# Gated attention with experts: other counts at which the scatters wait, the experts' count earlier, the variance's root earlier

## The chip, the core and the metric

The kernel runs on one core of one Trainium2 chip. The metric is the device time of one execution in microseconds (us). A core has TensorE (PE, matrix products), VectorE (DVE), ScalarE (ACT), GpSimd (POOL) and SyncE (SP), each with its own queue of instructions that run in order, and 16 DMA engines. Engines tell one another of finished work by semaphores.

## What is computed

The input x is 8 batches of 512 rows of 256. Attention here runs over the 256 features, not over the rows, and its result gates with a mixture of 32 experts, 6 of them for each row:

```
xn = layernorm(x)
q, k, v = xn Wq, xn Wk, xn Wv
scores  = einsum('bse,bsf->bef', q, k) / sqrt(8)       # 256 x 256 for each batch
s       = (softmax(scores) applied to v) Wo
logits  = xn gate_weight^T                             # 32 experts
        softmax; best 3 of 8 groups; best 6 experts of them; their weights normalised
y       = sum over a row's 6 experts of weight * (silu(xn w1^T) * (xn w3^T)) w2^T
shared  = (silu(xn sw1^T) * (xn sw3^T)) sw2^T
out     = x + s * silu(y + shared)
```

## The kernel before

There are two stages. In the first, a loop over the 8 batches computes the attention, the shared expert and the routing, and writes each normalised row to six places of a table in HBM, `slots_d`, sorted by expert. The second runs over pairs of pages of 128 such rows through the experts, gathers the results back and writes the output. The change touches the first stage only. Batches are numbered 0 to 7 here, as `b` in the code.

The order on every engine is written out by hand. TensorE's `batch(b)` (L736) runs, in this order: half of the shared expert's first layer (`shared_up(0)`, L718, semaphore `s_ab_ps`); the product A (L710, `s_a_ps`); `shared_up(1)`; the turning of the next batch's rows (`turn`, L685, `s_xt_ps`); the scores S (L710, `s_s_ps`); the next batch's logits (`gate`, L698, `s_lg_ps`); half of the shared expert's second layer (L726, `s_y_ps`); the product R (L710, `s_r_ps`), which waits for the softmax's weights (ACT, L533, `s_p`); the other half (L726, `s_y_ps`); the product M (L710, `s_m_ps`), which waits for ACT's copy of R (L602); the next batch's Gram matrix (`gram`, L732); `count(b + 1)` (L704 and L705, `s_cnt`), which counts the chosen experts of the next batch from `sel16`, VectorE's result of the routing (L920, `s_sel`); and last the attention's output (L726 into banks 2 and 3, `s_at_ps`), which waits for ACT's copy of M (L610).

VectorE's `batch(b)` (L1064): the shared expert's hidden values (L1044), the scores' maximum (L1068), the next but one batch's statistics (L877), then `route(b + 1)` (from L925, which waits for the logits), `split_low` (L995), `low_weights(b - 1)` (12 instructions on L1050), `spread_root(b + 2)` and `moved_mean` (L887 to L898, which finish the inverse root of the variance), `place(b + 1)` (from L949, which waits for `s_cnt`) and `weigh(b + 1)`. ScalarE normalises the next but one batch's rows (L527) as soon as L898 is done; those stand in its queue ahead of L610.

GpSimd issues the scatters, indirect DMAs of 128 rows each, on L487: 24 for each batch, 192 in all. It numbers those of one batch n = 0 to 23. Before some of them `let_pass(b, n)` (L463) waits until TensorE has reached a certain product. No data need these waits.

```
due = {4: (s_y_ps, 2 * b + 1), 7: (s_r_ps, b + 1), 9: (s_y_ps, 2 * b + 2),
       11: (s_m_ps, b + 1), 15: (s_at_ps, 2 * b + 2)}
if nxt:
    due.update({2: (s_lg_ps, b + 2), 13: (s_cnt, b + 2), 17: (s_ab_ps, HC * b + HC + 1),
                19: (s_a_ps, b + 2), 21: ...})
```

So ahead of scatter 7 of batch b, POOL waits for R of batch b. The ones at 17, 19 and 21 wait for products of the next batch.

## Time and profile before

| | us |
|---|---|
| median of 3 executions | 685.56 |
| lowest and highest | 684.07 and 687.75 |
| profiled execution, its time | 691.99 |
| profiled execution, its span | 690.2 |
| PE, DVE, ACT, POOL busy in the span | 548.6, 472.2, 359.1, 383.4 |

The profile is of one execution, whose own time lies 6.43 us above the median. Its span, 690.2 us, is what the trace covers; 1.8 us lie around it. Times in the rows are us from the span's start. The first stage ends on TensorE at about 304 us. In a row of the timeline, the number in brackets is how long the engine had been idle before the instruction, and behind the arrow stands what ended that; "remote" there means that a semaphore's update came at that moment, well after the instruction that made it had ended.

### The profile page before, as it was taken

To read this page: it belongs to the slowest core of one execution; us is meant where nothing else is said; L and a number is where in the kernel's file an instruction comes from. 1 tells how busy PE (TensorE), PEld (TensorE's weight loads), DVE (VectorE), ACT (ScalarE), POOL (GpSimd) and SP (SyncE) were. 2 spreads that over 40 slices of the span, in tenths; PEclk is the share of its full clock that TensorE was granted. 3 is DMA by queue.
4 is the path that set the end of the run, shared out by engine and by line. 5 is a ranking of instruction groups with operands and counts; after the bars stand their busy time and mean duration, and the time that the engine had idled before them with its cause. 6 is when DMAs were issued, how large, how long until landed. Compare 5 with 4: busy or idle time off the path is not lost.

```text
span 690.2 us, 14473 instructions
## 1 busy us (share of the span) xinstructions
PE 548.6 (79%) x4095; PEld 446.7 (65%) x4095; DVE 472.2 (68%) x1443; ACT 359.1 (52%) x606; POOL 383.4 (56%) x402
## 2 busy tenths in 40 slices
PE   7789696979697978437999889888888889888830
PEld 6566575756576765326999777777777777677620
DVE  6968687877788877722454567667677667667765
ACT  5546464546464644224655656556556556556421
POOL 1156667676666766753003556556565556565662
PEclk9889798998898999868999999999999999999975
DMA  9999996858393532754888888888888988888764
GB/s 320 416 354 347 366 334 227 285 214 298 130 334 113 207 117 91 230 150 122 201 217 262 290 280 283 280 280 285 290 272 292 279 279 267 290 276 286 226 198 141
DMA packets 111288, 174.80 MB, mean 253 GB/s; under 512 B 25072, under 2 KB 68848, under 8 KB 110320
## 3 DMA queue, kind: packets, MB, share of 16 engines
q1 hardware_dynamic: 87280, 108.29, 47.4%
q0 software_dynamic: 18432, 50.36, 23.2%
q10 hardware_dynamic: 5504, 15.24, 6.4%
q8 instruction: 40, 0.66, 0.4%
q14 instruction: 32, 0.26, 0.1%
HBM read 78.41 MB, written 92.27 MB: 247 GB/s over the span
## 4 chain that ended last, share of the span: by engine, by line
PE 53%; DVE 21%; issue 15%; another core or an unknown queue 6%; ACT 4%; DMA 1%; DVEq 0%; SPq 0%; ACTq 0%
PE ps L835 17%; PE ps L857 8%; PE ps L726 7%; PE ps L710 6%; PE ps L818 6%; PE ps L718 4%; DVE sw L1133 3%; PE ps L845 3%; PE ps L732 2%; DVE w_all L1050 2%; DVE work L1152 2%; DVE work L1159 1%; DVE stats L877 1%; DVE early L1141 1%
## 5 line engine op out<-in xcount | busy, mean ns | idle before, releaser
L508 POOL DMA_INDIRECT early<-slots_d,slot_at x192 | 186.6, 972 | 178.0 <-DMA slots_d<-early 56.6
L487 POOL DMA_INDIRECT slots_d<-early,slot_at x96 | 96.9, 1009 | 75.0 <-issue 25.7
L487 POOL DMA_INDIRECT slots_d<-work,slot_at x96 | 97.7, 1018 | 45.1 <-issue 26.5
L835 PE MATMUL ps<-w_all,xnT 128*128 x798 | 102.9, 275 | 15.9 <-issue 13.6
L835 PEld LDWEIGHTS ps<-w_all,xnT 128*128 128x128 f16 x798 | 71.4, 98 | 36.3 <-issue 24.6
L647 ACT ACTIVATE xnT<-ps 128x1024 f16<-128x1024 f16 x67 | 68.8, 1029 | 46.6 <-PE ps L818 28.0
L668 ACT ACTIVATE early<-ps 128x512 f32<-128x512 f32 x112 | 67.3, 602 | 46.6 <-remote 30.8
L818 PE MATMUL ps<-ident,work 128*128 128x128 f16 x796 | 66.7, 222 | 24.9 <-issue 24.8
L1159 DVE CAST work<-ps 128x256 f16<-128x256 f32 x75 | 31.6, 422 | 75.0 <-remote 45.0
L1133 DVE SCALAR_TENSOR_TENSOR sw<-early,wk,sw 128x256 f32<-128x256 f32 x160 | 77.7, 486 | 3.5
L818 PEld LDWEIGHTS ps<-ident,work 128*128 128x128 f16 x796 | 54.6, 99 | 28.8 <-issue 26.4
L653 ACT ACTIVATE work<-ps 128x256 f32<-128x256 f32 x112 | 43.9, 393 | 55.6 <-remote 37.9
L857 PE MATMUL ps<-w_all,work 128*128 x447 | 62.6, 277 | 0.9 <-issue 0.9
L1152 DVE SCALAR_TENSOR_TENSOR work<-ps,work 128x256 f32<-128x256 f32 x112 | 46.5, 416 | 20.4 <-ACT work L653 19.0
L710 PE MATMUL ps<-early,work 128*128 128x256 f32 x128 | 39.4, 462 | 25.8 <-ACT work L533 18.9
L835 PE MATMUL ps<-w_all,sw 128*128 x396 | 50.6, 274 | 8.3 <-issue 8.0
L710 PEld LDWEIGHTS ps<-early,work 128*128 128x128 f32 x128 | 28.6, 231 | 34.7 <-ACT work L533 21.0
L726 PE MATMUL ps<-work,early 128*128 128x256 f32 x128 | 34.7, 432 | 17.7 <-issue 13.8
L857 PEld LDWEIGHTS ps<-w_all,work 128*128 128x128 f16 x447 | 43.9, 99 | 6.3 <-issue 1.5
L835 PEld LDWEIGHTS ps<-w_all,sw 128*128 128x128 f16 x396 | 35.4, 98 | 18.6 <-issue 12.7
L647 ACT ACTIVATE sw<-ps 128x1024 f16<-128x1024 f16 x33 | 34.0, 1032 | 20.9 <-remote 15.4
L718 PE MATMUL ps<-xnT,sw 128*128 128x512 f16 x192 | 44.0, 379 | 0.0
(164 smaller groups left out, 989.4 us busy)
## 6 DMA issues: line engine op xcount, KB each, us to landing
slots_d<-early SPq DMA_DIRECT2D x112, 256.0 KB
work<-slots_d SPq DMA_DIRECT2D x100, 256.0 KB
slots_d<-pad SPq DMA_DIRECT2D x7, 3072.0 KB
w_all<-in_wexp ACTq DMA_DIRECT2D x7, 1536.0 KB
slots_d<-work SPq DMA_DIRECT2D x1, 5120.0 KB, 19.2
s_all<-in_x SPq DMA_DIRECT2D x8, 512.0 KB, 6.3
ysh_d<-work ACTq DMA_DIRECT2D x8, 512.0 KB
early<-ysh_d SPq DMA_DIRECT2D x32, 128.0 KB
```

The lines of the kernel that those rows point to most:

```text
L487: pool.indirect_dma_start(slots_d[:, :], bass.IndirectOffsetOnAxis(ap=slot_at[:, at:at + 1], axis=0), split[b % XN_RING][:, t, :], None).t ...
L508: pool.indirect_dma_start(gath[:, at % GATH_RING, :], None, slots_d[:, :], bass.IndirectOffsetOnAxis(ap=slot_at[:, rank_of(at):rank_of(at) ...
L647: act.activation(x_halves[n % 3], turned_pair(p), ACT.Copy).then_inc(s_eT, 1)
L668: act.activation(y_e[:, p % DEEP, :], ps[:, 2 + p % 2, :], ACT.Copy, scale=1.0 / W_UP).then_inc(s_ey, 1)
L710: mm = pe.matmul(ps[:, bank, m * H:(m + 1) * H], lhs[:, k, m * P:(m + 1) * P], rhs[:, k, :], start=(k == 0), stop=(k == HC - 1))
L718: mm = pe.matmul(ps[:, 4 + 2 * m + w, :], sw13[:, w_low, w, k, m * P:(m + 1) * P], xnT16[:, x_low, k, :], start=(n == 0 and k == 0), stop= ...
L726: mm = pe.matmul(ps[:, bank + n, t * H:(t + 1) * H], lhs[:, k, at:at + P], rhs[:, k, :], start=(k == 0), stop=(k == HC - 1))
L818: mm = pe.transpose(turned_pair(p)[:, at:at + P], slot16[:, at_slot(p) + h, low, c * P:(c + 1) * P], ident16[:])
L835: mm = pe.matmul(ps[:, 5 + p % 2, h * 2 * I:(h + 1) * 2 * I], turned_x(p)[:, x_low * HC + k, h * P:(h + 1) * P], w16[:, bass.ds(at + (w_lo ...
L857: mm = pe.matmul(ps[:, 2 + p % 2, h * H:(h + 1) * H], hT_e[p % 3][:, h_low, h, :], w16[:, bass.ds(at + (w_low * WEXP + HC * 2 * I), H)], s ...
L1133: dve.scalar_tensor_tensor(acc[:, k, :], gath[:, at % GATH_RING, :], wk[:, rank_of(at):rank_of(at) + 1], ysh_l[k] if at % TOP_K == 0 else ...
L1152: dve.scalar_tensor_tensor(h_e[p % 2], up(p)[:, :, 1, :], 1.0 / (X_UP * W_UP), silu_e[p % 2], ALU.mult, ALU.mult).then_inc(s_eh, 1)
```

## The change

Three places are edited. The waits of POOL's scatters get other counts: from batch 1 on there are six a batch instead of ten, for R, M, the attention's output, and the next batch's A, S and logits. In batch 0 the waits ahead of 17, 19 and 21 become one, for the second half of `shared_up` of batch 1. On TensorE `count(b + 1)` moves from behind the Gram matrix to ahead of M. On VectorE `low_weights` moves behind the variance's root.

```diff
-                nxt = b + 1 < B
-                due = {4: (s_y_ps, 2 * b + 1), 7: (s_r_ps, b + 1), 9: (s_y_ps, 2 * b + 2),
-                       11: (s_m_ps, b + 1), 15: (s_at_ps, 2 * b + 2)}
-                if nxt:
-                    due.update({2: (s_lg_ps, b + 2), 13: (s_cnt, b + 2), 17: (s_ab_ps, HC * b + HC + 1),
-                                19: (s_a_ps, b + 2), 21: (s_xt_ps, 2 * b + 6) if b + 2 < B else (s_a_ps, b + 2)})
+                if b == 0:
+                    due = {2: (s_lg_ps, 2), 4: (s_y_ps, 1), 7: (s_r_ps, 1), 9: (s_y_ps, 2), 11: (s_cnt, 2),
+                           13: (s_m_ps, 1), 15: (s_at_ps, 2), 17: (s_ab_ps, HC + HC)}
                 else:
-                    due[2] = (s_s_ps, b + 1)
+                    due = {3: (s_r_ps, b + 1), 7: (s_m_ps, b + 1), 13: (s_at_ps, 2 * b + 2)}
+                    if b + 1 < B:
+                        due[17] = (s_a_ps, b + 2)
+                if b + 1 < B:
+                    due[20] = (s_s_ps, b + 2)
+                if b + 2 < B:
+                    due[23] = (s_lg_ps, b + 3)
...
                 half_by_tile(1, 6, hT_s, sw2, s_y_ps)
+                if not last:
+                    count(b + 1)
                 pe.wait_ge(s_r, b + 1)
                 product(1, w_vT, r_s, s_m_ps)
                 if not last:
                     gram(b + 1, 0)
                     gram(b + 1, 1)
-                    count(b + 1)
...
                 split_low(b + 1)
-                if b >= 1:
-                    low_weights(b - 1)
                 if b + 2 < B:
                     spread_root(b + 2)
                     moved_mean()
+                if b >= 1:
+                    low_weights(b - 1)
                 place(b + 1)
```

POOL's queue before, from the first scatter of batch 2; the names behind "waits" are the semaphores that the instruction waits for (`s_split`, `s_pads2` and `s_slots` guard its data, the others stand there through `let_pass`):

```order
67 L487 DMA slots_d<-early,slot_at 28672x256 [waits s_split,s_pads2,s_slots]
68 L487 DMA slots_d<-early,slot_at 28672x256
69 L487 DMA slots_d<-early,slot_at 28672x256 [waits s_lg_ps]
70 L487 DMA slots_d<-early,slot_at 28672x256
71 L487 DMA slots_d<-early,slot_at 28672x256 [waits s_y_ps]
72 L487 DMA slots_d<-early,slot_at 28672x256
73 L487 DMA slots_d<-early,slot_at 28672x256 [waits s_split]
74 L487 DMA slots_d<-early,slot_at 28672x256 [waits s_r_ps]
75 L487 DMA slots_d<-early,slot_at 28672x256
76 L487 DMA slots_d<-early,slot_at 28672x256 [waits s_y_ps]
77 L487 DMA slots_d<-early,slot_at 28672x256
78 L487 DMA slots_d<-early,slot_at 28672x256 [waits s_m_ps]
```

The same place in POOL's queue of the changed kernel, from the scatter of batch 1 that waits for the logits; L490 is L487 of before:

```order
59 L490 DMA slots_d<-work,slot_at 28672x256 [waits s_lg_ps]
60 L490 DMA slots_d<-early,slot_at 28672x256 [waits s_split,s_pads2,s_slots]
61 L490 DMA slots_d<-early,slot_at 28672x256 x2
62 L490 DMA slots_d<-early,slot_at 28672x256 [waits s_r_ps]
63 L490 DMA slots_d<-early,slot_at 28672x256 x2
64 L490 DMA slots_d<-early,slot_at 28672x256 [waits s_split]
65 L490 DMA slots_d<-early,slot_at 28672x256 [waits s_m_ps]
66 L490 DMA slots_d<-early,slot_at 28672x256 x4
67 L490 DMA slots_d<-early,slot_at 28672x256 [waits s_split]
68 L490 DMA slots_d<-early,slot_at 28672x256 [waits s_at_ps]
69 L490 DMA slots_d<-early,slot_at 28672x256 x3
70 L490 DMA slots_d<-early,slot_at 28672x256 [waits s_a_ps]
```

R's wait moved from the eighth scatter of a batch to the fourth, M's from the twelfth to the eighth, and the logits' from the third of a batch to the last of the one before it.

VectorE's queue before, at the end of batch 1's part:

```order
179 L995 SCALAR_TENSOR_TENSOR early<-early 128x256 x4
180 L1050 SCALAR_TENSOR_TENSOR w_all<-w_all 128x256 x12
181 L887 RECIPROCAL rough<-std 128x4
182 L888 SCALAR_TENSOR_TENSOR newt<-rough 128x4
183 L889 SCALAR_TENSOR_TENSOR newt<-mv,newt 128x4
184 L890 SCALAR_TENSOR_TENSOR rstd<-newt,rough 128x4
185 L898 SCALAR_TENSOR_TENSOR shift<-mv,rstd 128x4
186 L947 MEMSET early 128x32
187 L949 COPY counts<-ps 128x4x32
```

And of the changed kernel:

```order
179 L999 SCALAR_TENSOR_TENSOR early<-early 128x256 x4
180 L891 RECIPROCAL rough<-std 128x4
181 L892 SCALAR_TENSOR_TENSOR newt<-rough 128x4
182 L893 SCALAR_TENSOR_TENSOR newt<-mv,newt 128x4
183 L894 SCALAR_TENSOR_TENSOR rstd<-newt,rough 128x4
184 L902 SCALAR_TENSOR_TENSOR shift<-mv,rstd 128x4
185 L1054 SCALAR_TENSOR_TENSOR w_all<-w_all 128x256 x12
186 L951 MEMSET early 128x32
187 L953 COPY counts<-ps 128x4x32
```

The five small instructions of the root now stand ahead of the twelve of the low weights; the copy of the counts keeps its place.

## Rows read from the trace of the kernel before

**Rows 1.** Windows, batches 1 to 6 and batch 7: busy us and instructions by engine.

```profile
54.30:263.00 208.70, 173.42 (x782) 133.10 (x781) 162.68 (x603) 114.11 (x181) 142.00 (x141) 0.89 0.71 244
263.00:304.40 41.40, 23.72 (x90) 16.78 (x88) 23.86 (x72) 15.14 (x20) 26.98 (x28) 0.79 0.54 171
```

**Rows 2.** Waits, 40 to 310 us: us in total, times, longest.

```profile
POOL slots_d L487 <- remote: 22.3, 11, 3.4
...
DVE counts L949 <- issue: 16.3, 5, 6.6
...
ACT early L527 <- DVE shift L898: 13.8, 5, 5.0
```

**Rows 3.** Timeline, batch 1, R and M: start, us, engine, line, [idle before].

```profile
71.49 1.99 PE L710 MATMUL ps<-early,work 128*128 128x256 f32 x8 [1.19 <-issue]
...
72.30 0.96 POOL L487 DMA_INDIRECT slots_d<-work,slot_at  x1 [0.30 <-issue]
...
74.15 0.29 DVE L920 TENSOR_TENSOR sel<-early 128x128 bf16<-128x128 f32 x1
...
76.16 1.04 POOL L487 DMA_INDIRECT slots_d<-work,slot_at  x1 [0.30 <-issue]
78.91 0.60 ACT L602 ACTIVATE work<-ps 128x512 f32<-128x512 f32 x1 [3.87 <-remote]
79.16 1.73 POOL L487 DMA_INDIRECT slots_d<-work,slot_at  x1 [1.96 <-remote]
...
79.56 3.78 PE L710 MATMUL ps<-work,early 128*128 128x256 f32 x8 [4.36 <-issue]
```

**Rows 4.** Timeline, batch 2, product R, POOL's stop ahead of scatter 7, product M.

```profile
106.94 2.42 PE L710 MATMUL ps<-early,work 128*128 128x256 f32 x8 [2.56 <-issue]
...
114.59 2.53 POOL L487 DMA_INDIRECT slots_d<-early,slot_at  x1 [1.83 <-remote]
...
115.00 3.62 PE L710 MATMUL ps<-work,early 128*128 128x256 f32 x8 [2.66 <-issue]
```

**Rows 5.** Timeline, batch 3, product M and the attention's output.

```profile
147.77 1.89 PE L710 MATMUL ps<-work,early 128*128 128x256 f32 x8
147.88 1.04 POOL L487 DMA_INDIRECT slots_d<-work,slot_at  x1 [0.31 <-issue]
...
156.43 0.96 POOL L487 DMA_INDIRECT slots_d<-work,slot_at  x1 [2.30 <-remote]
...
156.84 6.74 PE L726 MATMUL ps<-work,early 128*128 128x256 f32 x16 [3.61 <-ACT work L610]
```

**Rows 6.** Timeline, batch 4, the logits and product R.

```profile
172.93 1.87 PE L698 MATMUL ps<-g_w,early 128*128 128x32 f32 x16
173.13 0.96 POOL L487 DMA_INDIRECT slots_d<-work,slot_at  x1 [0.30 <-issue]
...
179.62 0.29 DVE L925 TENSOR_REDUCE row<-ps 128x4 f32<-128x128 f32 x1 [3.11 <-remote]
179.86 0.96 POOL L487 DMA_INDIRECT slots_d<-early,slot_at  x1 [1.97 <-remote]
...
183.04 3.78 PE L710 MATMUL ps<-early,work 128*128 128x256 f32 x8 [6.44 <-ACT work L533]
```

**Rows 7.** Timeline, batch 7 and the first pair of pages.

```profile
282.79 1.89 PE L710 MATMUL ps<-work,early 128*128 128x256 f32 x8
...
288.69 0.96 POOL L487 DMA_INDIRECT slots_d<-work,slot_at  x1 [0.30 <-issue]
...
298.07 0.95 POOL L487 DMA_INDIRECT slots_d<-work,slot_at  x1 [3.38 <-remote]
...
298.48 5.90 PE L726 MATMUL ps<-work,early 128*128 128x256 f32 x16 [13.80 <-issue]
...
312.21 1.86 PE L818 MATMUL ps<-ident,work 128*128 128x128 f16 x16 [7.72 <-issue]
...
316.77 0.96 POOL L487 DMA_INDIRECT slots_d<-work,slot_at  x1 [0.30 <-issue]
```

## The prediction

> **What bounds the kernel now.** Read the windows first. Batches 1 to 6 take 208.7 us, 34.8 us each; TensorE is busy for 173.42 of them, 28.9 a batch, so some 5.9 us a batch are holes in it [rows 1]. No other engine fills a batch either: VectorE is busy 27.1 us of it, ScalarE 19.0. POOL shows 142.00 us for 141 scatters, 1.007 us each, and between two that wait for nothing stand 0.30 us [rows 1, 3]. So 24 scatters need 24 x 1.31 = 31.4 us of a batch's 34.8: POOL has 3.4 us to spare and no more.
>
> Next the waits and the timeline, to see what the holes are. In the first stage POOL alone ends 11 waits, 22.3 us, on "remote" [rows 2], a semaphore that came long after its instruction. The reader is to compare three times in each stretch: when the product ended, when its reader started, and when POOL last stopped. In batch 1 the product R ended at 71.49 + 1.99 = 73.48. ScalarE, idle and next in line, copied it only at 78.91, 5.4 us later; POOL had issued scatters all the while, stopped at 77.20 for R's semaphore itself (its wait ahead of scatter 7), and the copy came 1.7 us behind that stop [rows 3]. Batch 2 repeats it: R ended at 109.36, POOL stopped at 112.76, went on at 114.59, M started at 115.00 after 2.66 us of idling [rows 4]. In batch 3 it is M: ended at 149.66, POOL stopped ahead of scatter 11 at 154.13, released at 156.43 [rows 5]. In batch 4 the logits: ended at 174.80, stop at 177.89, VectorE's first reader at 179.62 [rows 6]. In batch 7 M ended at 284.68, POOL stopped at 294.69 and was released at 298.07; TensorE idled 13.80 us [rows 7]. So **an update of TensorE's that falls into a run of scatters may be seen only 1.7 to 3.4 us after POOL stops**. It does not always happen: M of batch 2 is no such case. What `let_pass` sets is therefore where POOL stops, and the question is whether it stops before the product ends or after.
>
> TensorE also pays behind a hole: M took 3.78 and 3.62 us after holes of 4.36 and 2.66 [rows 3, 4] and 1.89 without one [rows 5], so it ran there at half of the full clock, 1.2 for 2.4 GHz. The attention's output took 6.74 us after 3.61 [rows 5]. The Trainium skill, in "TensorE: Matmul & The Clock Gate", part 1, says that the clock depends on how busy the array has been of late and falls to half when it idles. By that rule alone a closed hole gives more than its length; the trace agrees, with 3.78 against 1.89.
>
> **The change part by part.**
>
> *R's wait from scatter 7 to 3, M's from 11 to 7.* In batch 1 scatter 3 is the one at 72.30 [rows 3]; POOL would have stood still from 72.00, before R's end at 73.48. The hole of 4.36 closes and M runs at 1.89 instead of 3.78: 6.2 us. In batch 2 the stop moves four scatters, 5.2 us, ahead, from 112.76 to 107.5, before R's end: 2.66 + 1.73 = 4.4 us. In batch 3 scatter 6, at 147.88, would be the last and end at 148.92, before M's end at 149.66: the 3.61 close and 6.74 halves, 7.0 us. In batch 7 scatter 6 is the one at 288.69, so the stop comes at 289.65 instead of 294.69; M ended before either, so its update stays late, but by 5.0 us less [rows 7].
>
> *The logits' wait from scatter 2 of the next batch to 23.* In batch 4 scatter 22 is the one at 173.13; POOL would stop at 174.09, before the logits end at 174.80. VectorE's 3.11 us of idling go, and with them that much of TensorE's 6.44 [rows 6]: 3.1 us. Batches 5 and 6 I credit with nothing.
>
> These sum to 6.2 + 4.4 + 7.0 + 3.1 = 20.7 us ahead of batch 7 and 5.0 in it. But the sum assumes that POOL stays where it was, and it can't: it has only 3.4 us a batch, 20.5 us in six. Were TensorE to gain all of it, POOL would never be early for anything. **Counts against time** show where it would be late. From R to M TensorE needs two products at 1.89, 3.8 us, and POOL has four scatters to issue, 5.2 us: 1.5 us late. From S to the logits TensorE needs 1.87 us and POOL three scatters, 3.9 us: 2.1 late. Only from the logits to R, where TensorE waits for the softmax (from 174.80 to 186.8 in batch 4, and 8 to 9 us if nothing is late), does it have time to spare for four, 5.2 us. So some updates get caught as now, with 1.7 us behind the stop. Bounds for batches 1 to 6: 0, if each closed hole opens another, and 20.5. I take the middle, 10, since the rows show R certain to profit and M and the logits now and then. With 5.0 in batch 7 this is 15.
>
> *Waits removed (both for the shared expert's second layer, its first, the counts, the turned rows).* A wait that is passed costs nothing; one that stops POOL costs it up to 2.30 us [rows 5]. Their removal lets POOL run on over these signals. What they release (ScalarE's copy of the shared output, ahead of R's copy in its queue) must be out before R, and POOL now stops for R. Cost 0; bounds 2.3 us a batch either way, one such stop more or less. *The new wait for S* holds POOL at scatter 20 near the moment when S ends; behind it are queued only scatters, and behind their landing in the end the next but one batch's split rows (ScalarE L539). Cost 0, the same bounds.
>
> *The count between R and M.* Two small products move, with their wait for `s_sel`. Queued behind are M and all after it. In batch 1 `sel16` was ready at 74.44, and TensorE was through with what precedes the count at 79.56 - 4.36 = 75.20: a slack of 0.8 us [rows 3]. A faster R would eat it. Cost 0 to 1 us a batch; I take 0.5 in all, because M waits for R's copy anyway. The gain: VectorE waited 16.3 us in five batches for the counts [rows 2], 3.3 each. Its later results reach TensorE only through the hidden values and the next batch's scores; in the rows TensorE idles for ScalarE or a late semaphore. Gain 0 to 3.3 a batch; I take 0.5 in all.
>
> *The root ahead of the low weights.* ScalarE waited 13.8 us in five batches for it [rows 2], 2.8 each. No DMA moves with it. It feeds the next but one batch's rows; of TensorE's work it delays only the copy of M, queued behind, which the Gram matrix covers. Gain 0 to 2.8 a batch, taken as 0. The low weights come five small instructions later, and ScalarE needs them only at the batch's end: 0. If that cover is gone, the 2.8 are on the path and add to the gain.
>
> **Sum**: 691.99 - 15 + 0.5 - 0.5 = 677.0 for the profiled execution. It lies 6.43 us above the median 685.56. Nothing tells what these 6.4 are, but late updates are what can differ from one execution to the next at an unchanged program, so I expect the median execution to have a third fewer of them, and the change to give it two thirds: 10. That makes 675.6.
>
> **The rivals.** *POOL becomes the bound and it gets slower.* The mechanism is the late stop itself: each of the six waits that catches an update costs POOL about 1.9 us [rows 3, 4]. With n of them in a batch it takes 31.4 + 1.9 n. At n = 1.8 that is today's 34.8, the point from which it decides; at n = 3 it is 37.1, 2.3 more, 14 us in six batches. Less the 5 of batch 7 and a little elsewhere, 8 us: 693. For it: two of the six waits are late by the counts above, and 11 scatters instead of 9 remain behind TensorE's last product of the stage. Against it: today there are ten waits. Those two scatters, 2.6 us, end later than the 317.73 of now; the pairs of pages that need them come well behind the first at 312.21 [rows 7].
>
> *The waits don't matter.* Updates are late by chance, and moving a stop moves the chance. Then only VectorE's and ScalarE's edits are left, 0 to 2 us: 684. The Trainium skill, in "Advanced Engine Details and Errata", Miscellaneous Facts, gives 50 to 100 ns for a sequencer's reading of a semaphore. By that figure no product would be seen microseconds late and this rival would be right. The rows speak against it: in five stretches the delay ends 1.7 to 3.4 us behind POOL's stop, wherever that is.
>
> *All of it is gained*: 20.5 + 5.0, at two thirds 17, or whole 25.5: 660 to 668. It needs POOL never to wait in vain, and two of the counts speak against it.
>
> **How the numbers follow.** The forecast, 668 to 682, has 0.55; all of it 0.15; the waits don't matter, 682 to 689, 0.17; slower 0.13. Likeliest is 675.6. The range of 8 in 10 runs from 664 to 689, leaving out the slow case and the lower part of the best. A measurement of this kernel can tell about 0.5%, 3.4 us, from no change: faster 0.70, same 0.17, slower 0.13.
>
> **What would show it.** Right: the timeline has POOL idle ahead of scatter 3 when R ends, and ScalarE's copy of R within 0.3 us of that; M takes 1.9 us in most batches; batches 1 to 6 take near 33 us; TensorE's idling ahead of batch 7's output is 8 to 9 us instead of 13.80. Wrong: the holes ahead of M are closed but those ahead of the logits' or A's readers have grown; TensorE idles ahead of the moved count; batches stay at 34.8. The forecast fails if an update is held by something other than POOL's scatters.

## The result: no gain, slightly slower

The changed kernel takes 692.31 us (688.09 to 697.30, 22 runs), the kernel before beside it 689.20 us (684.07 to 694.95, 22 runs): ratio 1.0045, 95% interval 1.0023 to 1.0067. The forecast of 675.6 and its range, 664 to 689, both miss it. The profiled execution took 697.3 us, its span is 695.6; before it was 691.99 and 690.2. The profiled execution is the slowest of the 22, so the two profiles lie further apart (5.4 us) than the medians (3.1 us). Each profile is one execution; where a single hole falls can differ from one to the next.

### The profile after

Lines moved by 3 or 4: scatters are L490, products L713, halves of the outputs L729, the logits L701, the count L707, the first reader of the logits L929. First the windows of batches 1 to 6 and of batch 7 (us from and to, length, then busy us and instructions of TensorE, its weight loads, VectorE, ScalarE, POOL, then granted clock, DMA share, GB/s). They answer to [rows 1]:

```profile
55.70:265.20 209.50, 172.26 (x782) 132.93 (x781) 157.03 (x583) 113.51 (x180) 137.98 (x140) 0.89 0.70 239
265.20:304.30 39.10, 22.02 (x90) 15.19 (x88) 23.39 (x70) 15.52 (x21) 26.18 (x27) 0.83 0.57 178
```

The six batches take 209.5 us instead of 208.7, and the output ends at 304.3 as it did. The waits between 40 and 310 us (us in total, times, longest) answer to [rows 2]:

```profile
POOL slots_d L490 <- remote: 25.5, 15, 3.3
...
ACT s_all L622 <- remote: 19.4, 6, 5.1
...
DVE row L929 <- remote: 9.2, 3, 3.9
...
DVE mx L1072 <- remote: 8.2, 3, 3.3
...
ACT work L605 <- remote: 3.4, 1, 3.4
...
ACT early L530 <- DVE shift L902: 1.4, 2, 0.9
```

The same waits in the kernel before:

```profile
ACT work L602 <- remote: 9.9, 2, 6.0
...
DVE row L925 <- remote: 7.4, 3, 3.1
...
ACT s_all L619 <- remote: 2.3, 1, 2.3
```

VectorE's 16.3 us of waiting for the counts are down to 1.2, ScalarE's 13.8 for the root to 1.4: both edits do what they say. But VectorE now waits 21.0 us in seven stretches for ScalarE's part of the hidden values (L1048), where before it waited 0.5 us: its wait has moved as well. POOL's late releases went up, from 11 (22.3 us) to 15 (25.5). The late waits of others changed their place: ScalarE's for R (L602, now L605) fell from 9.9 to 3.4 us; those for the logits rose from 7.4 to 9.2, for S (the scores' maximum, L1072) from none to 8.2, and for the attention's output (L619, now L622) from 2.3 to 19.4. Now the timeline of batch 1, to be read beside [rows 3] (start, us, what, in brackets the idle time before and what ended it):

```profile
71.34 1.99 PE L713 MATMUL ps<-early,work 128*128 128x256 f32 x8 [2.50 <-issue]
...
76.53 0.23 PE L707 MATMUL ps<-sel,ones 128*128 128x128 bf16 x1 [1.47 <-DVE sel L924]
...
77.05 1.06 ACT L542 ACTIVATE early<-early 128x1024 f16<-128x1024 f32 x1 [5.76 <-DMA slots_d<-early,slot_at]
...
77.51 0.96 POOL L490 DMA_INDIRECT slots_d<-work,slot_at  x1 [2.14 <-remote]
...
79.13 2.56 PE L713 MATMUL ps<-work,early 128*128 128x256 f32 x8 [2.32 <-ACT work L605]
```

R ended at 73.33. POOL stood ahead of scatter 3 only from 77.51 - 2.14 = 75.37, and not from 72.00 as forecast, because its stops in batch 0 had grown and batch 1 began 3.3 us later on it. TensorE idled 1.47 us ahead of the moved count and 2.32 ahead of M, 3.8 us together instead of 4.36; M took 2.56 us instead of 3.78. Ahead of R's copy in ScalarE's queue stood L542, which waited until 77.05 for scatters to land. So in batch 1 the hole stayed. In batches 2 to 6 the hole ahead of M is gone. And this is what stands ahead of the next R, that of batch 2, to be read beside [rows 4]:

```profile
99.14 1.94 PE L701 MATMUL ps<-g_w,early 128*128 128x32 f32 x16
...
104.09 0.96 POOL L490 DMA_INDIRECT slots_d<-work,slot_at  x1 [0.30 <-issue]
...
105.92 0.29 DVE L929 TENSOR_REDUCE row<-ps 128x4 f32<-128x128 f32 x1 [3.91 <-remote]
106.16 0.96 POOL L490 DMA_INDIRECT slots_d<-work,slot_at  x1 [1.11 <-remote]
...
109.34 3.78 PE L713 MATMUL ps<-early,work 128*128 128x256 f32 x8 [6.46 <-issue]
```

The logits ended at 101.08. POOL issued scatters until 105.05, stopped ahead of scatter 23, and VectorE read them at 105.92, 4.8 us late and 0.9 us behind the stop. R waited 6.46 us (2.56 before) and ran at 1.2 GHz, 3.78 us. Over batches 1 to 6, TensorE's holes ahead of the count, M and the attention's output fell from 12.0 us to 3.8; those ahead of or within the logits and ahead of R rose from 23.3 to 33.4. The balance, 2.0 us more, is TensorE's idle time in the windows (208.70 - 173.42 = 35.3 us and 209.50 - 172.26 = 37.2). Its busy time fell by 1.2 us, so the six batches grew by 0.8. **The holes moved from one product to another.**

In batch 7, beside [rows 7]:

```profile
284.33 1.99 PE L713 MATMUL ps<-work,early 128*128 128x256 f32 x8 [0.71 <-issue]
...
291.90 0.96 POOL L490 DMA_INDIRECT slots_d<-work,slot_at  x1 [0.30 <-issue]
295.87 0.60 ACT L601 ACTIVATE work<-ps 128x512 f32<-128x512 f32 x1 [11.59 <-remote]
296.21 0.96 POOL L490 DMA_INDIRECT slots_d<-work,slot_at  x1 [3.35 <-remote]
...
299.01 5.32 PE L729 MATMUL ps<-work,early 128*128 128x256 f32 x16 [12.69 <-ACT work L613]
```

M ended at 286.3. POOL stopped for it at 292.9; the updates were seen 3.0 us later, at 295.9, when ScalarE could start on the copies ahead of M's in its queue. The stop came 1.8 us earlier than before (294.7), not 5.0, since POOL began the batch 3.3 us later. The hole shrank from 13.80 to 12.69.

Where are the 5.4 us by which the span grew? Not ahead of the output's end (304.4 and 304.3). Behind it the last scatter ended at 320.2 instead of 317.7, ScalarE's first SiLU of the experts came at 321.2 instead of 319.0, POOL's first gather at 373.9 instead of 369.8: 4.1 us of the 5.4; the other 1.3 fell behind that. The start of the experts' stage in the changed kernel (first product, POOL's last scatter, first SiLU):

```profile
314.23 2.30 PE L839 MATMUL ps<-w_all,xnT 128*128 x12 [0.45 <-issue]
...
319.23 0.96 POOL L490 DMA_INDIRECT slots_d<-work,slot_at  x1 [0.30 <-issue]
321.16 0.38 ACT L656 ACTIVATE work<-ps 128x256 f32<-128x256 f32 x1 [4.96 <-remote]
```

And in the kernel before, where the last scatter is the one at 316.77 [rows 7]:

```profile
314.53 2.47 PE L835 MATMUL ps<-w_all,xnT 128*128 x12 [0.45 <-issue]
...
318.96 0.66 ACT L653 ACTIVATE work<-ps 128x256 f32<-128x256 f32 x2 [2.46 <-PE ps L835]
```

The first product ended 0.5 us earlier (316.5 instead of 317.0), and its reader started 2.2 us later: 4.6 us late instead of 2.0, and in both kernels 1.0 to 1.2 us behind the last scatter's end. Behind POOL's last stop no stop follows in that run of scatters, so this too is a late update.

### The profile page after: what moved, and what is told of

Its sections match the earlier page's. It is cut to its first block, busy times and chain, and to the rows that moved or that the text cites. A ratio compares the mean times of both kernels' runs of the same rounds, so it can differ in the third digit from the quotient of the medians.

```text
span 695.6 us, 14473 instructions
## 1 busy us (share of the span) xinstructions
PE 554.7 (80%) x4095; PEld 443.7 (64%) x4095; DVE 469.5 (67%) x1443; ACT 358.4 (52%) x606; POOL 379.3 (55%) x402
## 4 chain that ended last, share of the span: by engine, by line
PE 49%; DVE 16%; issue 14%; another core or an unknown queue 11%; ACT 8%; DMA 1%; DVEq 0%; ACTq 0%
PE ps L839 18%; PE ps L861 8%; PE ps L713 6%; PE ps L729 5%; PE ps L822 5%; PE ps L735 4%; DVE sw L1137 4%; PE ps L849 3%; ACT w_all L561 2%; DVE work L1156 2%; DVE work L1163 1%; PE ps L721 1%; ACT L582 1%; DVE stats L881 1%
## 5 line engine op out<-in xcount | busy, mean ns | idle before, releaser
L490 POOL DMA_INDIRECT slots_d<-early,slot_at x96 | 95.4, 993 | 77.8 <-issue 25.6
L839 PE MATMUL ps<-w_all,xnT 128*128 x798 | 107.5, 276 | 29.6 <-issue 23.1
L490 POOL DMA_INDIRECT slots_d<-work,slot_at x96 | 96.5, 1005 | 47.5 <-issue 26.5
L839 PEld LDWEIGHTS ps<-w_all,xnT 128*128 128x128 f16 x798 | 69.8, 98 | 52.0 <-issue 38.8
L822 PE MATMUL ps<-ident,work 128*128 128x128 f16 x796 | 61.9, 222 | 7.5 <-issue 7.5
L713 PE MATMUL ps<-early,work 128*128 128x256 f32 x128 | 40.7, 474 | 29.7 <-ACT work L536 20.7
L839 PE MATMUL ps<-w_all,sw 128*128 x396 | 52.9, 277 | 8.9 <-issue 8.6
L1156 DVE SCALAR_TENSOR_TENSOR work<-ps,work 128x256 f32<-128x256 f32 x112 | 46.3, 413 | 16.7 <-issue 15.2
L713 PEld LDWEIGHTS ps<-early,work 128*128 128x128 f32 x128 | 29.6, 239 | 39.0 <-ACT work L536 23.7
L839 PEld LDWEIGHTS ps<-w_all,sw 128*128 128x128 f16 x396 | 33.8, 99 | 23.9 <-issue 15.7
L849 PE MATMUL ps<-ident,work 128*128 128x128 f32 x223 | 44.0, 278 | 3.2 <-issue 3.2
L729 PE MATMUL ps<-work,early 128*128 128x256 f32 x128 | 30.6, 395 | 12.7 <-ACT work L613 12.7
```

Of the source, the lines that this page charges most:

```text
L490: pool.indirect_dma_start(slots_d[:, :], bass.IndirectOffsetOnAxis(ap=slot_at[:, at:at + 1], axis=0), split[b % XN_RING][:, t, :], None).t ...
L713: mm = pe.matmul(ps[:, bank, m * H:(m + 1) * H], lhs[:, k, m * P:(m + 1) * P], rhs[:, k, :], start=(k == 0), stop=(k == HC - 1))
L729: mm = pe.matmul(ps[:, bank + n, t * H:(t + 1) * H], lhs[:, k, at:at + P], rhs[:, k, :], start=(k == 0), stop=(k == HC - 1))
L822: mm = pe.transpose(turned_pair(p)[:, at:at + P], slot16[:, at_slot(p) + h, low, c * P:(c + 1) * P], ident16[:])
L839: mm = pe.matmul(ps[:, 5 + p % 2, h * 2 * I:(h + 1) * 2 * I], turned_x(p)[:, x_low * HC + k, h * P:(h + 1) * P], w16[:, bass.ds(at + (w_lo ...
L849: mm = pe.transpose(turned_hidden(p)[:, h * P:(h + 1) * P], h_e[p % 2][:, h, :], ident[:])
```

## Experiments

The kernel before takes 689.7 us on the chip of the first runs and 694.8 to 696.4 on three others, but 590.1 and 589.4 on two. Ratios are always to the kernel before on the same chip. That difference was not foreseen and turned out useful: in the eight traces taken on the 590-us chips no wait ends on "remote", so no update of TensorE's is late there. The kernel before was timed on those chips but not profiled.

### The parts alone

The waits alone are the new `let_pass` in the kernel before; the count alone is

```
                 half_by_tile(1, 6, hT_s, sw2, s_y_ps)
+                if not last:
+                    count(b + 1)
                 pe.wait_ge(s_r, b + 1)
...
-                    count(b + 1)
```

and the root alone moves `low_weights(b - 1)` behind `spread_root(b + 2)` and `moved_mean()`.

> The kernel before with the new counts of the scatters' waits alone. Theory A (late updates only change their place: the holes ahead of M close, those ahead of R and the logits' readers open, and two more scatters are left behind the last product of the first stage, so that the first pairs of pages wait for them): all of the change's loss is here, ratio 1.003 to 1.007, and the profile has M's holes under 1 us in batches 1 to 6 and R's at 5 to 6 us. Theory B (the moved count or the moved root is what costs): ratio under 1.001.

> The kernel before with the experts' count ahead of M alone. Theory A: within 0.2% of before, since M waits for ScalarE's copy of R anyway; VectorE's waits for the counts shrink from 3.3 us each to under 1. Theory B (TensorE stands idle for sel16 ahead of the count, and M, Gram and all behind it come later): 1.5 us in each of 7 batches, ratio 1.005 or more.

> The kernel before with the variance's root ahead of the low weights alone. Theory A: within 0.2% of before; ScalarE's waits for the root fall from 2.8 us each to under 1, and nobody waits for what ScalarE does there. Theory B: the low weights, 1 us later, hold the high weights at the batch's end and so the next batch: ratio over 1.003.

Measured (kernel before 689.70): waits 694.36, 1.0070 (1.0041 to 1.0100); count 689.63, 0.9999 (0.9973 to 1.0025); root 687.83, 0.9970 (0.9939 to 1.0001). The sum of the three, +0.4%, is the whole change's 1.0045. The loss is the waits', and the root may have gained 0.3%, which its interval just fails to show. The ratio of the waits alone is at the top edge of theory A; the profile is only in part what that theory said: M still had holes of 4.1 and 2.8 us in batches 1 and 5, and R's were 0.9 to 6.2.

The profile of the waits alone holds a surprise. Its output ends at 292.9, 11 us earlier than before, and its first transposes of pages (L821) still come at 311.7, against 312.2 before:

```profile
293.24 0.27 PE L794 MATMUL ps<-ident,table 128*1 128x128 f32 x1 [0.36 <-DVE table L1032]
...
303.80 0.23 DVE L1037 CAST early<-ps 1x76 int16<-1x76 f32 x1 [8.69 <-remote]
...
311.70 1.86 PE L821 MATMUL ps<-ident,work 128*128 128x128 f16 x16 [18.19 <-issue]
```

The turned table of experts (L794), which every page's product needs, was ready at 293.5 and seen at 303.8. POOL, being behind, found the output's semaphore already there and made no stop. So a TensorE that is ahead of POOL makes the stops vanish that let its updates through.

### Does POOL hold the updates?

The kernel before without any wait in `let_pass` (nothing that is computed is left out), and the changed kernel with the old waits, so with count and root alone:

```
             def let_pass(b, n):
+                pass
...
-                if n in due:
-                    pool.wait_ge(*due[n])
```

> The kernel before without any of let_pass's waits. Theory L (updates of TensorE are held while POOL issues scatters, and the stops let them pass): holes of 10 us and more in every batch, over 750 us. Rival W (the waits are only a cost; updates are late by chance): POOL's last scatter ends some 20 us sooner, and the time falls to 670 or is unchanged.

> The changed kernel with all of its scatters' waits as before: the moved count and the moved root together. If the parts add: 0.9999 x 0.997, ratio 0.994 to 1.000, and the changed kernel's 1.0045 is the waits' 1.007 less the root's 0.003. If the count costs once the root is early: over 1.000.

These fell on a 590-us chip: no waits 588.27, 0.9964 (0.9948 to 0.9981); old waits 591.37, 1.0008 (0.9987 to 1.0029). The first again, on a chip with 696.43:

> The same kernel without any of let_pass's waits, meant for the chip on which the kernel before takes 690 us (on the one where it takes 590 no update came late). Theory L (there updates of TensorE are held while POOL issues scatters, and stops let them pass): holes of 10 us and more in most batches, over 720 us. Rival W (late by chance, the waits only cost): 680 us or less.

802.41 us, 1.1519 (1.1428 to 1.1610). Its waits, whole span:

```profile
POOL slots_d L477 <- DVE slot_at L979: 152.8, 8, 25.8
...
PE ps L700 <- ACT work L592: 61.8, 5, 17.4
```

Without a stop TensorE idles up to 17.4 us ahead of M (L700) and 20.0 ahead of the attention's output, and POOL then waits for a batch's addresses, 11.9 to 21.1 us in each of seven batches (the 25.8 is the wait at the start, 25.6 in the kernel before). The same edit gains 0.4% where the kernel before takes 590. So the late updates are real, belong to POOL's runs of scatters, occur on some chips only, and `let_pass` is worth 15% there. This part of the prediction's reasoning stands. What in a run of scatters holds an update (POOL itself or the transfers that it starts) is not shown. The old waits with the new count and root once more on a chip with 589.41:

> The changed kernel with all of its scatters' waits as before, for a chip of 690 us. If the parts add, 0.9999 x 0.997: ratio 0.994 to 1.000. If the root's gain was chance: 0.999 to 1.003.

591.55, 1.0029 (1.0016 to 1.0043): no gain from the two edits there. It was meant for a 690-us chip; there count and root together were not run.

### Which of the moved waits?

Two kernels, one with batch 0's table as before, the other with the last batch's as before, the rest as changed:

```
                 if b == 0:
-                    due = {... 9: (s_y_ps, 2), 11: (s_cnt, 2),
-                            13: (s_m_ps, 1), 15: (s_at_ps, 2), 17: (s_ab_ps, HC + HC)}
+                    due = {... 9: (s_y_ps, 2), 11: (s_m_ps, 1), 13: (s_cnt, 2),
+                           15: (s_at_ps, 2), 17: (s_ab_ps, HC + 1), 19: (s_a_ps, 2), 21: (s_xt_ps, 6)}
...
+                if b == 1:
+                    due[2] = (s_lg_ps, 3)
...
+                if b == B - 1:
+                    due = {2: (s_s_ps, B), 4: (s_y_ps, 2 * B - 1), 7: (s_r_ps, B), 9: (s_y_ps, 2 * B),
+                           11: (s_m_ps, B), 15: (s_at_ps, 2 * B)}
```

> The changed kernel with batch 0's waits as before, again for the chip of 690 us. Theory P (3 us of the loss are POOL's stop ahead of scatter 17 of batch 0): ratio 0.998 to 1.001. Theory Q (the waits for S and the logits cost): 1.004 or more. Where no update is late, as on the chip of 590 us, it was 1.0058.

> The changed kernel with the waits of the last batch as they were before (M's ahead of scatter 11 instead of 7, the output's ahead of 15 instead of 13). Theory A (the scatters left at the end delay the first pairs of pages): M's update comes up to 5 us later, but four scatters more are out by then; the first pair's updates are seen 2 to 4 us sooner counted from the stage's last product. Net ratio to before 0.998 to 1.004. If the stage's last hole alone counted (the reason of the prediction), it would be 5 us slower than the changed kernel: 1.011.

1.0071 (1.0034 to 1.0108; 703.54 against 696.43) and 1.0065 (1.0034 to 1.0096; 694.57 against 689.70): the loss stays with either, so neither end alone makes it; no run has both as before. The first is no clean test of batch 0: its stops sum to 7.4 us instead of 12.2, but batch 1, with the logits' stop ahead of scatter 2 and R's ahead of 3, stood 10.9 us instead of 4.3. (The first of the two was 1.0058, 594.21, on a 590-us chip. A table with fewer stops, ahead of 2, 5, 11, 15 and 19, was expected to give 0.985 to 1.000 and gave 1.0160, 600.29, there: POOL's stops summed to 20.2 us beyond the usual 0.30, 12.4 of them from batch 1 on, against 7.9 and none with the old waits on that chip.)

Then the two halves of the change apart, in batches 1 to 6: R, M and the output at 3, 7 and 13, the waits for the shared layer's second products and the counts gone, the others as before; and S at 20 instead of the turned rows at 21 and the logits at 23, with R and M as before.

```
+                if 1 <= b < B - 1:
+                    due = {2: (s_lg_ps, b + 2), 3: (s_r_ps, b + 1), 7: (s_m_ps, b + 1), 13: (s_at_ps, 2 * b + 2),
+                           17: (s_ab_ps, HC * b + HC + 1), 19: (s_a_ps, b + 2), 21: due[21]}
```

> The kernel before, with R's wait ahead of scatter 3, M's of 7 and the output's of 13 in batches 1 to 6, and the waits for the shared layer's second products and the counts gone there; logits, A and the turned rows as before. Where updates come late (690 us). Theory E (stopping earlier for R and M costs POOL its idling between the logits and R without an earlier R): ratio 1.004 to 1.008. Theory S (the stops for S and the logits cost): 0.995 to 1.002.

> The kernel before, with the turned rows' wait ahead of 21 replaced by S ahead of 20, and the logits' wait moved from scatter 2 to scatter 23 of the batch before. Theory S (two stops 1.9 us apart on TensorE with three scatters of 3.9 us between make the logits late each time, so the holes ahead of R are 5 to 6 us): ratio 1.004 to 1.008. Theory E: 0.997 to 1.002.

On a chip with 589.41 they gave 592.06, 1.0035 (1.0015 to 1.0054), and 593.93, 1.0084 (1.0054 to 1.0115): where nothing is late a stop only costs. The first half again, on a chip with 694.77:

> The kernel before with only the waits of R and M (and of the attention's output, 15 to 13) moved in batches 1 to 6 to scatters 3 and 7; the logits' wait stays at scatter 2, and all that were there before remain. The prediction's sum gave these two waits 17.6 us. Theory A (only POOL's total counts): R and M holes smaller, but the last scatter and the whole within 0.5% of before, or slower by up to 0.5% if POOL idles more. Theory B (it is the logits' and S's waits that spoil the change): faster by 1 to 2.5%, 0.975 to 0.99, where the kernel before takes 690; no gain where it takes 590.

717.88 us, 1.0312 (1.0234 to 1.0389): neither theory's number. (The text above says that all other waits remain; in the kernel the three ahead of 4, 9 and 13 are gone.) R and M early, which by the sum of their parts were to bring 17.6 us, cost 23. Batch 1's end in it:

```profile
96.80 1.94 PE L701 MATMUL ps<-g_w,early 128*128 128x32 f32 x16 [0.83 <-ACT early L547]
...
105.84 0.96 POOL L490 DMA_INDIRECT slots_d<-early,slot_at  x1 [0.30 <-issue]
109.05 0.29 DVE L928 TENSOR_REDUCE row<-ps 128x4 f32<-128x128 f32 x1 [9.38 <-remote]
109.29 0.96 POOL L490 DMA_INDIRECT slots_d<-early,slot_at  x1 [2.49 <-remote]
```

The logits ended at 98.74, when 19 of the batch's scatters were out; before it were 21 to 23. The stop for them stands ahead of scatter 2 of the next batch, and they were seen at 109.05, 10.3 us late; so in each of five batches, 9.6 to 10.3 us late (VectorE's waits for it are 9.4 us at most, 37.6 in all), and TensorE idled 8.8 to 10.5 us ahead of R. POOL, stopped again one scatter later for R itself, stood there for 4.3 to 6.3 us. Its stops in batches 1 to 6 sum to 49.4 us beyond the usual 0.30, instead of 23.1. An earlier stop moves TensorE ahead of POOL for all that comes after. The waits alone, which have stops at 20 and 23, cost 0.7% instead of 3.1% (on another chip, and with other tables in batches 0 and 7), so those stops seem to mend most of this, and not all: S ends when 17 to 19 of POOL's scatters are out instead of 19 to 22, and its stop is at 20. S and the logits early were not run on such a chip, so what that half does alone there is open.

### What takes the gain at the end?

Without the last eight scatters of the last batch (those eight row groups are left out of the computation):

```
+                        if b == B - 1 and t * TOP_K + k >= 16:
+                            continue
```

> The kernel before without the last 8 of batch 7's 24 scatters; their rows are missing from the table. Theory P (the first pairs' updates are held till POOL's last scatter ends, so the experts' stage starts by that and not by TensorE's last product): ScalarE's first silu follows the last scatter by 1 to 2 us still, up to the 10 us that TensorE needs behind its last product, and the time falls by 3 to 6 us, ratio 0.991 to 0.996. Rival (only pairs from the 15th on need those scatters, the reason of the prediction): 0.999 to 1.001.

> The kernel before, but the last eight scatters of the last batch are left out (its last batch stores only 16 of its 24 row groups). Where the kernel before takes about 690 us its last scatter ended at 317.7 us and the first SiLU came at 319.0. Theory A (the experts' first pairs see their signals only once POOL's last scatter is out, so POOL's total sets the start): last scatter and first SiLU both 9 to 11 us earlier, the whole 8 to 10 us shorter, ratio 0.985 to 0.989. Theory B (TensorE's output at 304 us and the transposes behind it set the start, POOL's tail is hidden): first SiLU within 2 us of 319, ratio 0.997 to 1.000. Where the kernel before takes about 590 us both expect no change: there the first SiLU stands ahead of the last scatter already.

On the chip with 589.41: 590.46, 1.0004 (0.9987 to 1.0020). On that with 694.77: 694.16, 0.9985 (0.9956 to 1.0014). Eight scatters fewer gain nothing that can be told from noise, though the last one now ends at 306.5 instead of 317.7 and the first SiLU comes at 315.7 instead of 319.0. The theory that the last scatter alone sets the start falls. The trace shows what remains:

```profile
296.80 0.27 PE L793 MATMUL ps<-ident,table 128*1 128x128 f32 x1
303.41 0.60 ACT L621 ACTIVATE s_all<-ps 128x512 f32<-128x512 f32 x1 [7.54 <-remote]
303.44 0.23 DVE L1036 CAST early<-ps 1x76 int16<-1x76 f32 x1 [5.72 <-remote]
303.65 2.86 POOL L489 DMA_INDIRECT slots_d<-work,slot_at  x1 [2.32 <-remote]
...
310.58 1.87 PE L820 MATMUL ps<-ident,work 128*128 128x128 f16 x16 [13.51 <-issue]
```

The table, ready at 297.1, was seen at 303.4, at POOL's stop ahead of scatter 15. Does that stop decide, then? The last batch's stops were moved, in the kernel before with the root's edit:

```
                 else:
-                    due[2] = (s_s_ps, b + 1)
+                    due = {0: (s_y_ps, 2 * B - 1), 2: (s_r_ps, B), 4: (s_m_ps, B), 8: (s_at_ps, 2 * B), 9: (s_table_ps, 1),
+                            16: (s_eT_ps, 1), 19: (s_eab_ps, 1)}
```

with the second line of waits in the second kernel only (it relies on the first pair not needing the last batch).

> Only the root's move, and in the last batch alone other stops: ahead of scatter 0 (shared output's first half), 2 (R), 4 (M), 8 (the attention's output), 9 (the turned table of experts) instead of 2, 4, 7, 9, 11, 15. The batches before are as in the kernel before. Theory C (what decides is when the turned table of the experts is seen, and that is at POOL's stop in the last batch: 304.5 us before, 304.5 after, 303.8 with the waits alone, although TensorE was through at 304.4, 304.3 and 292.9): TensorE waits 2 to 5 us instead of 13.8 ahead of the output, table seen near 294 instead of 304.5, first transposes 7.7 us later near 302, the first SiLU 307 to 314, whole 5 to 11 us shorter, ratio 0.984 to 0.993 where the kernel before takes 690. Theory D (the end hangs on POOL's count of scatters and gathers): the last scatter stays within 3 us of 318 and so does the whole, 0.996 to 1.002. Where the kernel before takes 590 no update is late: 0.998 to 1.008, the stops only hold POOL.

> As early_last, with two more stops in the last batch, ahead of scatter 16 for the first pair's transposes and of 19 for its first product, so that these are seen while scatters are still left. Theory C: the first SiLU comes 4 to 5 us behind the first transposes (5.1 where no scatter followed, 6.8 to 9.9 where some did), 2 to 4 us earlier than in early_last, the whole 0 to 4 us shorter than that. Theory D: both equal. A stop ahead of 16 may hold the last scatter by up to 3 us; the kernel before with eight scatters fewer was not faster, so that costs nothing.

697.75 us, 1.0022 (0.9993 to 1.0050), and 696.55, 1.0019 (0.9990 to 1.0049), beside 694.87. The places moved the way theory C said, though not as far: the hole ahead of the output 1.5 us instead of 13.80, the table seen at 298.5 and 297.8 (near 294 was expected), the first transposes at 306.1 and 305.5, 6 us earlier (near 302), the SiLU at 316.5 and 313.8 (307 to 314). The time did not: it is that of theory D, whose last scatter, at 320.5 and 320.0, came out too. From the second kernel:

```profile
313.75 0.38 ACT L654 ACTIVATE work<-ps 128x256 f32<-128x256 f32 x1 [3.98 <-remote]
314.00 0.96 POOL L488 DMA_INDIRECT slots_d<-work,slot_at  x1 [0.48 <-remote]
...
322.32 2.50 SPq L403 DMA_TRANSPOSE work<-slots_d  x2
322.33 0.38 ACT L654 ACTIVATE work<-ps 128x256 f32<-128x256 f32 x1 [8.19 <-remote]
...
323.51 0.82 PE L836 MATMUL ps<-w_all,work 128*128 x3 [6.02 <-DVE work L1153]
```

The first SiLU was let through by the new stop (POOL went on at 314.00). The next one and the next pair's load (SyncE's transposing DMA, which waits for a product's semaphore) came at 322.3, 2.3 us behind the last scatter's end at 320.0, and TensorE idled 6.02 us. From there to 372 it was busy without a hole. So **two chains meet at the experts' start**: table, first transposes, SiLU; and the last scatter. The time of POOL's first gather shows it. With two distances chosen to fit these traces, 51.2 us behind the first SiLU and 52.5 behind the last scatter (in the kernel before they are 50.9 and 52.1), the later one gives:

| kernel | table seen | first SiLU | last scatter ends | the later gives | first gather |
|---|---|---|---|---|---|
| before | 304.5 | 319.0 | 317.7 | 370.2 | 369.8 |
| changed | 304.5 | 321.2 | 320.2 | 372.7 | 373.9 |
| waits alone | 303.8 | 321.6 | 317.0 | 372.8 | 375.1 |
| count alone | 301.4 | 316.1 | 314.6 | 367.3 | 367.0 |
| root alone | 301.1 | 316.3 | 314.3 | 367.5 | 367.1 |
| eight scatters fewer | 303.4 | 315.7 | 306.5 | 366.9 | 366.9 |
| early stops | 298.5 | 316.5 | 320.5 | 373.0 | 374.7 |
| early stops, two more | 297.8 | 313.8 | 320.0 | 372.5 | 372.8 |
| R and M early | 329.7 | 344.3 | 342.9 | 395.5 | 395.6 |
| batch 0 as before | 306.2 | 323.7 | 323.2 | 375.7 | 376.1 |
| last batch as before | 308.6 | 323.2 | 321.8 | 374.4 | 374.1 |

The fit is within 2.3 us. The SiLU alone would miss by 7.0 and 7.9 us in the two kernels with early stops, the last scatter alone by 5.6 in the waits alone and 7.9 with eight scatters fewer. The two distances were read off these traces and not set by an experiment of their own, so the rule is a summary of them, not a proof.

Why does the last scatter count? Not for its data. On the 590-us chips the pairs don't wait for it. The changed kernel with the old waits there:

```profile
277.92 0.38 ACT L653 ACTIVATE work<-ps 128x256 f32<-128x256 f32 x1 [0.80 <-PE ps L836]
...
282.75 2.58 SPq L403 DMA_TRANSPOSE work<-slots_d  x2
...
286.91 0.96 POOL L487 DMA_INDIRECT slots_d<-work,slot_at  x1 [0.30 <-issue]
...
329.10 0.98 POOL L508 DMA_INDIRECT early<-slots_d,slot_at  x1 [41.23 <-DMA slots_d<-early]
```

SiLU and the next pairs' loads run while scatters are still issued, the last of which ends at 287.9. In all eight traces of these chips the first gather lies within 1.1 us of 51.2 us behind the first SiLU, although in seven of them the last scatter ends 5.8 to 13.3 us behind that SiLU. So on the 690-us chips the last scatter counts because it ends a run of scatters without a stop, behind which the first pairs' updates are seen. To gain there, an edit must bring both forward: the last scatter's end, which is POOL's sum of scatters and stops, and the table. From the first gather to the end of the span pass another 318 to 325 us, different from one execution to the next, more than the change itself moved.

## Why the prediction was wrong, step by step

*Late updates.* Right in kind: without stops the time is 15% longer. The distance of 1.7 to 3.4 us behind POOL's stop was too narrow; the logits of batch 2 in the changed kernel were seen 0.9 us behind it. The Trainium skill, in "Advanced Engine Details and Errata", Miscellaneous Facts, gives 50 to 100 ns for reading a semaphore; on the 690-us chips these runs differ, with 4.8 us from the logits' end to their reader and 10.3 us for the table in the waits alone; on the 590-us chips nothing speaks against it.

*R's and M's waits earlier.* From batch 2 on the holes ahead of M and the output closed as forecast. In batch 1, credited with 6.2 us, the hole stayed (4.36 against 1.47 + 2.32), since POOL's stop came at 75.37 and not at 72.00. The credit failed. The step that failed is that the middle of "0, if each closed hole opens another, and 20.5" was taken, 10 us; batches 1 to 6 grew by 0.8 us, so the lower bound was the result. The text had the reason, S to the logits "2.1 late", but counted lateness at fixed places. An earlier stop shifts TensorE against POOL, so S ended when 17 to 19 scatters were out, and the logits of batch 2 were seen 4.8 us late where the count had 2.1 us. The lateness in the middle of the batch moved to its end; R and M early alone show it undiluted, +3.1%.

*The logits' wait.* Credited with 3.1 us in batch 4; there the hole of 6.44 us ahead of R moved ahead of the logits themselves (5.7 us). Nothing gained.

*Batch 7.* 5.0 us were forecast; the stop came 1.8 earlier and the hole shrank by 1.1. Even the whole would likely have brought nothing: the early stops closed it, and the time stayed.

*"11 instead of 9 scatters behind the last product ... the pairs that need them come well behind the first": cost 0.* This is the second step that failed. As to the data it holds: on the 590-us chips the first pairs run before the last scatter is out. But it left out the prediction's own rule. Eleven scatters without a stop hold the updates of the first pairs: the first product of the experts was seen 4.6 us late instead of 2.0. The last scatter ended 2.5 us later, the first SiLU 2.2, the first gather 4.1. The prediction never asked what happens behind the output, where a gain made before it has to arrive. Those two scatters are not the whole loss: with the last batch's stops as before it stayed (1.0065).

*New S wait, removed waits.* Put at 0; POOL's stops beyond the usual 0.30 us grew from 36.3 us (24 stops) to 41.6 (28), most of it in batch 0 (8.7 to 12.2). Batch 0 was changed by more than the one wait that the text on the change names: M's wait moved from 11 to 13, the count's from 13 to 11, and S and the logits were added at 20 and 23; the sum has no term for it. The new stop ahead of 17 alone took 4.5 us. With batch 0 as before the loss stayed, but that run has its own long stop in batch 1, so no single one of them is shown to be the cause.

*Count and root.* Right within their bounds: count 0.9999; root 0.9970, where 0 to 2.8 us a batch had been taken as 0. The slack ahead of the count was eaten as the text feared, but once only, with 1.47 us of idling in batch 1.

*The rivals.* The slower one was priced at 693, 0.7 us from the measurement, but by luck and not for its reason: batches 1 to 6 grew by 0.8 us, not 14, and POOL's stops there and in batch 7 by 1.8. "The waits don't matter" falls by the 15%. *Carrying the execution to the median* at two thirds changed nothing in the sign. The median of three that it started from, 685.56, lies 3.6 us under that of the 22 runs, 689.20, so part of the 16.7 us by which 675.6 was missed is the start and not the change.

## What to carry to other kernels

When a stop is moved so that one signal is seen in time, work out anew where the two engines stand against each other at every later signal of the loop; the lateness otherwise only changes its place. Before a gain is credited, follow it to the next stage and list what else that stage's start waits for: with two chains of nearly equal length (here the table, and the last scatter that ends a run without stops) a gain in one is worth little, and an edit must shorten both. A kernel that needs stops on one chip pays for them on another, so both kinds are to be measured.

## What the hardware showed that was not expected

The same program takes 589.4 and 590.1 us on two chips, 689.7 to 696.4 on four. The scatters themselves cost the same: from the first one's start to the last one's end, less the stops, POOL took 252.7 us in the kernel before on a 690-us chip and 251.4 in the one with the old waits on a 590-us chip. Between these two traces, 99.8 us apart, 40.7 lie ahead of the first gather and 59.1 behind it. From 320 us on, six of the 690-us trace's largest groups of waits of VectorE and ScalarE end on "remote", 166.6 us together; in the other there is none. So the difference is in the late updates and goes on in the experts' stage, where POOL gathers. A stretch of 50 us there, the kernel before on a 690-us chip and, under it, the one with eight scatters fewer on the 590-us chip (columns as above):

```profile
370.00:420.00 50.00, 44.40 (x449) 38.13 (x446) 28.43 (x70) 28.12 (x49) 29.77 (x31) 1.00 0.87 277
```

```profile
370.00:420.00 50.00, 50.00 (x534) 46.13 (x533) 43.65 (x108) 37.85 (x63) 38.42 (x39) 1.00 1.01 350
```

TensorE is busy 44.4 us of 50 and POOL issues 31 gathers, against 50.0 and 39; the granted clock is full in both. The two windows are at the same time but not at the same work, since gathers begin at 329 us in the second; in the first 50 us from its own first gather the old waits' trace has 50.00 and 38. With no gathers running TensorE is busy 49.66 of 50 on the 690-us chip too:

```profile
320.00:370.00 50.00, 49.66 (x498) 44.92 (x499) 24.73 (x64) 28.96 (x51) 0.18 (x1) 1.00 0.80 203
```

What differs between the chips, and why an update is let through now and then without a stop (at 300.85 and 303.80 in the kernel with the waits alone, at 316.5 with the early stops), stays open. Nothing here beats the kernel before for certain; the root's move alone, 0.9970 (0.9939 to 1.0001), comes nearest.
